# Four ScalarE copies of the turned row maxima become one VectorE multiplication with a table of ones and zeros

## What is computed

```python
q = einsum('bqm,muh->bquh', xn, Wq) + bq        # 32 heads of 64
k = einsum('bkm,mvh->bkvh', xn, Wk) + bk        # 8 heads, each used by 4 query heads
v = einsum('bkm,mvh->bkvh', xn, Wv) + bv
q, k = rope(q) * SCALE, rope(k) * SCALE
scores = where(abs(i - j) <= 128, q @ k.T, -1e9)
combined = concatenate([scores, sink_logits], -1)
probs = softmax(combined, -1)[..., :-1]
s = einsum('bquh,uhm->bqm', probs @ v, Wo) + bo
x = x + s * silu(fp8_quantised(xn) @ W_ffn.T + bias)
```

## Time and profile before

| | |
|---|---|
| median of 3 runs | 1925.35 us (1925.3 to 1928.68) |
| span of the profiled execution | 1928.5 us |
| TensorE busy (PE) | 1818.4 us, 94% |
| weight loads (PEld) | 1707.6 us, 89% |
| VectorE busy (DVE) | 1373.2 us, 71% |
| ScalarE busy (ACT) | 1406.3 us, 73% |
| GpSimd busy (POOL) | 1183.6 us, 61% |
| chain that ended last | PE 86%, DVE 5%, issue 4%, ACT 1% |

### The profile page before, as it was taken

How to read it: one execution, slowest core, us unless ns; L and a number is a source line. 1 busy time by engine, 2 the same in 40 slices (tenths; PEclk the granted TensorE clock), 3 DMA queues, 4 the chain that set the end, 5 groups by cost and what they waited for, 6 DMA issues and landing times.

```text
span 1928.5 us, 48655 instructions
## 1 busy us (share of the span) xinstructions
PE 1818.4 (94%) x13199; PEld 1707.6 (89%) x13199; DVE 1373.2 (71%) x4883; ACT 1406.3 (73%) x3764; POOL 1183.6 (61%) x1511
## 2 busy tenths in 40 slices
PE   3499999999999999999999999999999999999997
PEld 2399998999989999899989999899998999889996
DVE  8776776777767777767767777577777676776775
ACT  3277777777767777777867777677877787777775
POOL 4465656666566666666656666566666665665654
PEclk9699999999999999999999999899999999999999
DMA  5200000000000000000000000000000000000000
GB/s 191 82 8 2 0 1 25 12 2 0 13 20 5 1 0 18 19 2 0 1 19 18 2 0 1 30 7 2 0 18 19 2 1 1 18 24 2 0 1 17
DMA packets 20889, 28.07 MB, mean 15 GB/s; under 512 B 1344, under 2 KB 19264, under 8 KB 20544
## 3 DMA queue, kind: packets, MB, share of 16 engines
q1 hardware_dynamic: 20672, 25.45, 4.0%
HBM read 21.25 MB, written 4.19 MB: 13 GB/s over the span
## 4 chain that ended last, share of the span: by engine, by line
PE 86%; DVE 5%; issue 4%; ACT 1%; DMA 0%; DVEq 0%; POOLq 0%; POOL 0%; ACTq 0%
PE pv_bank L1042 26%; PE ring L974 15%; PE ring L1016 10%; PE acc L1063 9%; PE score L1028 8%; PE score L1030 7%; PE ring L983 5%; PE ring L1051 3%; PE ring L995 2%; PE ring L964 1%; PE ring L1001 1%; DVE junk L772 1%; DVE neg_max L781 1%; DVE sink_arg L786 1%; DVE proj L760 1%
## 5 line engine op out<-in xcount | busy, mean ns | idle before, releaser
L1042 PEld LDWEIGHTS pv_bank<-v,stage 128*128 128x128 f32 x5136 | 682.5, 192 | 4.7 <-issue 1.1
L1042 PE MATMUL pv_bank<-v,stage 128*128 128x65 f32 x5136 | 674.0, 266 | 0.9 <-DVE o_norm L800 0.9
L772 DVE CUSTOM_DVE_ANT_0 junk<-ring,mask 128x384 bf16<-128x384 f32 (+1 forms) x1036 | 507.0, 490 | 224.9 <-PE ring L1016 198.3
L529 ACT ACTIVATE stage<-score 128x512 f32<-128x512 f32 x640 | 357.0, 588 | 283.1 <-PE score L1030 282.3
L464 POOL TENSOR_SCALAR_AFFINE_SELECT stage<-stage 128x512 f32<-128x512 f32 x384 | 243.2, 641 | 425.1 <-ACT stage L529 425.1
L1016 PE MATMUL ring<-kT_high,qT_full 128*128 128x384 f32 (+1 forms) x1036 | 398.9, 385 | 16.6 <-DVE proj L760 15.4
L444 POOL TENSOR_TENSOR qk_parts<-turned,qk_parts 128x320 fp32r<-128x320 f32 x263 | 227.3, 864 | 207.0 <-ACT qk_parts L564 207.0
L552 ACT ACTIVATE qT_high<-ring,own_rows 8x128 fp32r<-8x128 f32 x1032 | 284.9, 345 | 13.7 <-PE ring L1001 7.3
L1028 PE MATMUL score<-qT_full,kT_high 128*128 128x512 f32 x640 | 267.7, 418 | 16.1 <-issue 14.9
L760 DVE TENSOR_TENSOR proj<-ring,bias 128x384 f32<-128x384 f32 x264 | 145.7, 552 | 183.7 <-PE ring L974 183.2
L1030 PE MATMUL score<-qT_high,kT_low 72*128 72x512 f32 x640 | 256.3, 400 | 0.0
(11 more groups left out here) (110 smaller groups left out, 3282.4 us busy)
## 6 DMA issues: line engine op xcount, KB each, us to landing
x_in<-in_x SPq DMA_DIRECT2D x13, 512.0 KB, 3.6
x_res<-in_x SPq DMA_DIRECT2D x18, 256.0 KB, 3.3
out<-x_res SPq DMA_DIRECT2D x16, 256.0 KB, 2.2
stage<-in_w_qkv SPq DMA_DIRECT2D x4, 768.0 KB, 5.0
gate<-in_x SPq DMA_DIRECT2D x4, 512.0 KB, 4.1
stage<-in_w_o SPq DMA_DIRECT2D x4, 512.0 KB, 3.6
bias<-in_b_qkv SPq DMA_DIRECT2D x1, 1152.0 KB, 6.6
bias<-in_b_qkv SPq DMA_DIRECT2D x1, 384.0 KB, 7.8
```

What stands on the lines that cost most here:

```text
L529: nc.scalar.activation(prob[:, q % 2 * 3 + n, :], score[(FIRST[q] + n) % 2][:, :], ACT.Exp) \
L772: nc.vector.tensor_tensor_reduce(junk[:, h % 2, 0:cols], ring[h % 2][:, 0:cols], mask[:, m0:m0 + cols], 1.0, LOWEST, ALU.add, ALU.max, row ...
L1042: last = nc.tensor.matmul(pv[:, h, :], prob[:, q % 2 * 3 + n, h * P:(h + 1) * P], v[:, par, k, :], start=(n == 0), stop=(n == len(BLOCKS[q ...
```

## The change

`max_rows` moves from ScalarE to VectorE and becomes one `tensor_tensor` multiplication of 8x512: the 8x128 rows in `ring[2]`, repeated for four heads, times `own_rows`, repeated along the 128 columns. On ScalarE only the sink's weight stays; it now waits for `s_neg_done` instead of `s_max_turned_pe`. VectorE runs the multiplication between `projected` and max 0, except at q = 1 and at q = 0 of k = 6, where it stands between max 0 and max 1. TensorE's order is unchanged.

```diff
-            def max_rows(b, q, par):
-
-                at(act, s_max_turned_pe, TILES, b, q + 1)
-                for h in range(GROUP):
-                    last = nc.scalar.activation(qT_high[D:D + NR, q, h * P:(h + 1) * P], ring[2][0:NR, 0:P],
-                                                ACT.Copy, scale=own_rows[:, h:h + 1])
-                last.then_inc(s_max_rows_done, 1)
+            def sink_weight(b, q, par):
 
+                at(act, s_neg_done, TILES, b, q + 1)
                 nc.scalar.activation(sink_exp[:, par, q, :], sink_arg[:, q, :], ACT.Exp).then_inc(s_sink_done, 1)
...
-                        max_rows(*back(it + 1, q, 2), 1 - par if q >= 2 else par)
+                        sink_weight(*back(it + 1, q, 2), 1 - par if q >= 2 else par)
...
+            def max_rows(b, q):
+
+                at(dve, s_max_turned_pe, TILES, b, q + 1)
+                nc.vector.tensor_tensor(qT_high[D:D + NR, q, :].rearrange("r (h n) -> r h n", h=GROUP),
+                                        ring[2][0:NR, 0:P].rearrange("r (a n) -> r a n", a=1)
+                                        .broadcast_to([NR, GROUP, P]),
+                                        own_rows[:, :].rearrange("r (h a) -> r h a", a=1)
+                                        .broadcast_to([NR, GROUP, P]), ALU.mult).then_inc(s_max_rows_done, 1)
...
+                    rows_new = (b if q >= 2 else c) is not None
+                    rows_late = q == 1 or (k, q) == (KV - 2, 0)
+                    if rows_new and not rows_late:
+                        max_rows(*back(it + 1, q, 2))
                     for h in range(GROUP):
+                        if rows_new and rows_late and h == 1:
+                            max_rows(*back(it + 1, q, 2))
```

## The result

The changed kernel takes 2037.19 us (median of 4 runs, 2029.09 to 2041.59) against 1925.32 for the kernel before in the same sequence of runs: a ratio of 1.0553, with a 95% interval of 1.0502 to 1.0603. The sign was as forecast, the size was not: 112 us were lost where 77 had been worked out, and 2037 lies above the range of 1962 to 2020. The profiled execution spans 2039.6 us.

What follows compares the result with a forecast made beforehand. TensorE's stream was taken as the bound: 5.0 us for four ordinary steps and 4.5 for the other four make 9.5 per batch, 76 in eight, some 1 at the start; 1925.35 + 77 is about 2002 us, range 1962 to 2020.

Steps and rivals of the forecast that it cites:

- The bound: TensorE's own stream, busy 94% of the span, sets the end; ScalarE is off the path, freeing it buys almost nothing.
- The duration and the join: VectorE's multiplication takes 0.69 us per tile and overlaps neither neighbour, with 0.03 us gaps on both sides.
- full overlap: Rival: VectorE's multiplication overlaps both neighbours by 0.08 us, costing 0.65 us per ordinary step, 40 us in all: 1965; chance 0.17.
- ScalarE's gaps: Gaps of 0.03 us around ScalarE's copies to other partitions, taken as the guide for VectorE's multiplication.
- The sum of an ordinary step: TensorE's added waits in k = 3: 0.6, 0.33, 0.15 and 0.17 us for q = 0 to 3, together 1.25.
- The removal's gain: Dropping ScalarE's copies (284.9 us) gives only 0.1 us in q = 3 tiles, at L1051, swallowed by the new wait.
- How the numbers follow: The prediction's paragraph of chances: forecast without overlap 0.64, overlap 0.17, slow handover 0.12, hiding 0.04, clock 0.03.
- handover: Rival: max 1 at q = 1 starts 0.20 us after the multiplication, not 0.03, 11 us more: 2013 to 2033; chance 0.12.
- The clock rival: TensorE's granted clock drops for one stretch per batch after the new waits, 64 us on top; chance 0.03.
- my 77: Total loss forecast: 9.5 us per batch, 76 in eight batches, and some 1 us for the start's three tiles.

Runs made afterwards that it cites:

- m1: The changed kernel moved by 32 instructions, its multiplication writing to a scratch tile from partition 0, row maxima left out of the scores: 1.0159 of the kernel before.
- m5: The changed kernel moved by 34 instructions, halves of qT_high and kT_low exchanged so the multiplication writes from partition 0, result whole: 1.0096 of the kernel before.
- e1: The changed kernel with 32 semaphore increments on VectorE ahead of its loops, nothing else: 1999.7 us, 1.0343 of the kernel before.
- m3: The changed kernel moved by 32 instructions, without the multiplication (row maxima left out of the scores), so the removal alone: 1918.55 us, 0.9949 of the kernel before.
- e6: The changed kernel with 19 semaphore increments on VectorE ahead of its loops: 1996.9 us, 1.0341 of the kernel before.
- e5: The changed kernel with 18 semaphore increments on VectorE ahead of its loops: 2051.3 us, 1.0629 of the kernel before.
- e2: The changed kernel with 8 semaphore increments on VectorE ahead of its loops: 2035.6 us, 1.0555 of the kernel before.
- e3: The kernel before, with its ScalarE copies, plus 16 semaphore increments on VectorE ahead of its loops: 1970.4 us, 1.0192 of the kernel before.

## Why the prediction was wrong, and where it was right

- **The bound** was right. ScalarE's freed 285 us bought little, and each wait put into TensorE's stream was paid.
- **The duration and the join** were right: 0.68 us for 0.69, gaps of 0.03 on both sides. m1 and m5 turn the rival "full overlap" on by the output's partition alone. With overlap m5 came out at 1948 us where that rival had 1965. The model of the Trainium skill, "VectorE: DVE Perf Modes", section "Two Vector instructions with no wait between them", that the prediction cited agrees in both directions (gaps of 0.03 us with the output at partition 64, overlaps of 0.09 and 0.07 with it at 0), and ScalarE's gaps had been a fair guide to VectorE.
- **The sum of an ordinary step** was right. Without the stall (e1 against before) k = 3 has 0.62 at q = 0, 0.34 at q = 1, 0.27 at q = 2 and 0.16 at q = 3, where the sum had 0.6, 0.33, 0.2 and 0.17; k = 2 has 1.07 in all. The loads' waits for maxima are 70.7 us, 221 times (70.1 in the changed kernel). e1 against m3, the multiplication without the removal, is 76 us by the ratios, where the sum had 77.
- **The removal's gain** was mis-sized. 0.1 us in some tiles was all that the earlier trace rows offered, and it was swallowed in the sum; m3 measured 10 us in all, since I had looked only at who waits for qT_high. The waits of L1016 for proj in k = 6, q = 2 were in the trace, but had no link to the copies that I could see. By steps, about half of what lies between the 66 us of e1 and my 77 stands in k = 6, which lost 0.8 us and not 1.4; most of the rest in k = 0 and 1, which lost 0.8 and 0.9 instead of 1.2 and 1.1.
- **The step that failed** is the sum's silent premise that VectorE gets one more instruction per tile and nothing else. "How the numbers follow" lists bounds for overlap, length, handover and clock, and none for the code itself. The loop grew from 274 to 282 instructions and began 10 later. So it reached over an edge of the fetched code, and its jump back waited 2.9 us in every batch. By the table of steps this cost 42 us with what followed from it, and the edge at 703 another 6. Less the 3.6 us by which e1's padding delays the first score product (from 96.7 to 100.3), and some 2 us by which its k = 6 is longer, this is the 41.7 us by which the profiled spans of the changed kernel and of e1 differ; one instruction of padding more or less (e6 against e5) makes such a distance come and go.
- **The clock rival** (0.03) happened in part, but not for its reason. The waits of 0.3 to 0.6 us left the granted clock alone, as the earlier trace rows had suggested; the fall to 0.50 came behind the stall of VectorE, which left TensorE idle for 1.7 us out of 4, in every batch. The rival was priced on its own and not as the second half of something else that delays TensorE by more than a tile's slack.
- Could it have been foreseen? The trace of before has the hints: the outer loop's jump back, with 838 instructions in its body, costs 2.7 to 3.1 us each time, the inner loop's, with 274, 0.3. With the edges known, counting places 547 and 820 between them, with 10 instructions of room. But the edges were found only by laying later traces over each other; that the trace of before alone would have given them is not shown. So the risk and its price could have been seen, as a rival of its own, and not which way it would fall. The rule of the Trainium skill, "Runtime: NRT & Kernel Launch", section "Instruction fetch mechanics", bears on exactly this; for a price the outer loop's jump has one.

## What to carry over

When a change adds instructions to a loop, count that engine's instructions from the loop's first to its jump back, and where they lie between the edges seen in the trace. A jump that costs 0.3 us and one that costs 3 can be one instruction apart, and a few increments ahead of the loop move it, for up to 5 us once here. Give an instruction between two others an output that starts at their partition. And place it by what stands behind the wait: the cheapest place for the multiplication was not a later one but the engine's idle time ahead of proj, and it took a reordering on another engine to open it.

## What the runs showed of the hardware

- VectorE's jump back took 0.3 us in the four kernels whose loop lay within three pieces of 128 instructions and 2.7 to 3.2 in the four where it reached into a fourth. Behind such a wait the first edge cost 2.3 us where it lay one instruction behind the target (e5), 1.2 and 1.0 where it lay 11 and 13 behind (e2, e3), and nothing more than in the first pass where it lay 18 behind (the changed kernel).
- An edge every 128 instructions costs VectorE's stream about 0.36 us even in straight code; ahead of proj in k = 3 and 5 it cost 0.36 us of TensorE's time.
- The multiplication and its neighbours on VectorE overlap by 0.07 to 0.09 us, with all outputs starting at partition 0, and stand 0.03 apart with its output at 64: 0.2 us for an instruction between two others, 35 to 48 us of this kernel's time (m1 and m5 against e1, by their ratios).
- After TensorE had idled 1.7 us out of 4 the granted clock of the changed kernel was 0.50 for some 10 us in five batches and for some 3 us in three (the 0.59 and 0.56 above are stretches that it fills in part).
- GpSimd's L444 and VectorE's L692, started within 0.02 us of each other, didn't run side by side at full speed: one of them took its usual time (0.86 or 0.43 us) and the other 1.13 or 1.15.
